# An attention stage's row sums: from sum products on TensorE to ScalarE's accumulator output, with their inverses spread by one product

## The chip, the cores and the metric

The kernel runs on one core of one Trainium2 chip. The metric is the device time of the whole launch in microseconds, the median of several runs. The core's engines are TensorE (PE; its weight loads are listed as PEld), VectorE (DVE), ScalarE (ACT), GpSimd (POOL) and SyncE (SP). Each works through its own queue in order, and they wait for each other by semaphores only.

## The reference

128 images of 176 x 208 pixels become 11 x 13 = 143 patches each, and with a class token S = 144 tokens of 128 features. Two layers follow. The first is a gated convolution and scan, then a mixture of 8 experts (two per token). The second is attention in a window of 32 tokens to each side, 8 heads of 16 features, and one of 16 experts per image. The change concerns the attention:

```python
valid = (idx >= 0) & (idx < S)
scores = jnp.einsum('bshd,bswhd->bshw', q, k_win) * scale
scores = jnp.where(valid[None, :, None, :], scores, -1000000000.0)
attn = jax.nn.softmax(scores, axis=-1)
out = jnp.einsum('bshw,bswhd->bshd', attn, v_win).reshape(B, S, D)
return out @ w_out + b_out
```

The softmax divides each row of exponentials by its sum. Everything is computed in float32.

## The kernel before

The kernel has three stages, one after the other: the first layer up to the routing (to about 1200 us of the profile), the experts' blocks (to about 1880 us), and the third stage, which gathers the experts' results, does the attention and the last experts. The change is in the third.

The third stage goes through the images in 32 steps of 4 images (576 tokens). It is a pipeline written out by hand: `step(v, w, x, y, z)` holds the work of five successive groups of images, each further along. `x` is the group whose attention begins, `y` the one whose attention ends, `v` and `w` are ahead of it (gather, sum and two normalizations, which end in `xq`, the attention's input), `z` is behind it. Each engine has its own `step`, and the order of the calls in it is the order on that engine.

The attention of a group is cut into NU = 9 units of 4 blocks of 16 queries. The 128 partitions of a score tile are 8 heads x 16 queries of a block; its 80 columns are the keys. A unit u goes through these steps:

- GpSimd `diagonal(u)` spreads the queries by head parity (`qdiag`, ring of 3).
- TensorE `scores(u)` (L1540, 16 small products, then the mask by L1548 and L1550) into one of two score banks.
- VectorE `minimum(u)` (L1836) takes the row minimum of the negated scores, `smin`.
- ScalarE `exps(u)` (L1752) makes 4 exponentials of 128 x 80, one per block.
- TensorE `turn(u)` (L1557) transposes them, 4 products; ScalarE `turned(u)` (L1760) copies them to `ex_t` (ring of 3).
- TensorE `values(u)`: 8 products with `pair_ones` (L1570) that sum the exponentials over the keys into `sum_bank`, and then the products with `val` (L1582) into `pv_bank`. Both lie in one PSUM bank, VB.
- VectorE `halves(u)` (L1843 the reciprocal `inv` of the sums, L1844) and `heads(u)` (L1848 `one_head`, L1851 `att`) pick the right half by parity and scale.

Each matmul in float32 appears as two records in the profile. `head_step` counts three VectorE steps per unit, the last of them `one_head`; `values(u)` waits until those of unit u-1 are done, since it writes the bank that they read. Units 0 to 5 of group `x` get their products in its own step, 6 to 8 in the next (as `y`).

GpSimd also issues 12 gathers per step between the `diagonal` calls (L1451), multiplies the gathered rows by the routing weights (L1459) and adds them (L1464, `ysum`). TensorE turns `ysum` (L1510) for `w`'s `prec`. On VectorE the small steps of `pick_expert` (L1959 to L1972) choose `y`'s expert of 16; ScalarE's L1780 makes 4 x 16 exponentials with an accumulator output for it.

## Time and profile before

| what | us |
|---|---|
| median of 3 runs (lowest, highest) | 3124.59 (3123.58, 3134.05) |
| the profiled execution, whole | 3155.56 |
| its span, first to last instruction | 3153.7 |
| TensorE busy in the span | 2771.0 (88%) |
| VectorE busy | 1942.3 (62%) |
| ScalarE busy | 1818.7 (58%) |
| GpSimd busy | 1283.4 (41%) |

Busy time is time in which an engine ran an instruction; waiting on a semaphore is not in it. In the timeline's rows the first number is the start in microseconds from the span's start, the second the time covered, and in brackets stands how long the engine was idle before, and what ended it. "issue" there is time in which the engine waited for nothing that the profile shows. The granted clock is a share of TensorE's full clock.

### The profile page before, as it was taken

To read this page: it belongs to the slowest core of one execution; us is meant where nothing else is said; L and a number is where in the kernel's file an instruction comes from. 1 tells how busy PE (TensorE), PEld (TensorE's weight loads), DVE (VectorE), ACT (ScalarE), POOL (GpSimd) and SP (SyncE) were. 2 spreads that over 40 slices of the span, in tenths; PEclk is the share of its full clock that TensorE was granted. 3 is DMA by queue.
4 is the path that set the end of the run, shared out by engine and by line. 5 is a ranking of instruction groups with operands and counts; after the bars stand their busy time and mean duration, and the time that the engine had idled before them with its cause. 6 is when DMAs were issued, how large, how long until landed. Compare 5 with 4: busy or idle time off the path is not lost.

```text
span 3153.7 us, 84405 instructions
## 1 busy us (share of the span) xinstructions
PE 2771.0 (88%) x30287; PEld 2124.4 (67%) x30287; DVE 1942.3 (62%) x4491; ACT 1818.7 (58%) x3661; POOL 1283.4 (41%) x1252
## 2 busy tenths in 40 slices
PE   6989899989989984999999948888888888888897
PEld 4666666666666663999999936666666666666665
DVE  4788888888777885222222215666666666666665
ACT  4767777767676773444444425555555555555554
POOL 1365555565555555000000045445454444555540
PEclk9999999999999996999999969999999999999998
DMA  3122222222222212777777721111111111111110
GB/s 125 68 92 84 81 80 75 75 91 84 80 81 75 75 31 64 228 230 227 230 229 228 228 75 38 47 46 45 44 44 44 44 44 44 44 45 44 44 34 28
DMA packets 139575, 284.62 MB, mean 90 GB/s; under 512 B 25440, under 2 KB 82784, under 8 KB 135392
## 3 DMA queue, kind: packets, MB, share of 16 engines
q1 hardware_dynamic: 114912, 245.68, 24.3%
q0 software_dynamic: 24576, 37.80, 4.5%
q8 instruction: 53, 0.87, 0.1%
q14 instruction: 34, 0.28, 0.0%
HBM read 215.08 MB, written 68.29 MB: 90 GB/s over the span
## 4 chain that ended last, share of the span: by engine, by line
PE 40%; DVE 8%; issue 7%; POOL 3%; DMA 1%; another core or an unknown queue 1%; ACT 1%; DVEq 0%; SPq 0%; POOLq 0%; ACTq 0%
PE psum L1154 9%; PE psum L1145 8%; PE psum L1540 4%; PE psum L1499 4%; PE psum L1570 2%; PE psum L1582 2%; DVE c L1964 2%; PE psum L1557 2%; PE psum L1516 2%; PE psum L1524 2%; POOL ycho L1451 2%; PE psum L1504 1%; PE psum L1550 1%; PE psum L1136 1%; DVE inv L1843 1%
## 5 line engine op out<-in xcount | busy, mean ns | idle before, releaser
L1451 POOL DMA_INDIRECT ycho<-expert_out,place x384 | 359.3, 936 | 668.5 <-DVE place L1829 585.0
L1019 POOL DMA_INDIRECT expert_in<-rows,slot_i x384 | 445.7, 1161 | 132.3 <-issue 111.5
L1188 ACT ACTIVATE hid<-psum,w_blk 128x256 f32<-128x256 f32 x608 | 268.9, 473 | 326.5 <-PE psum L1145 326.5
L1752 ACT ACTIVATE ex<-psum,smin 128x80 f32<-128x80 f32 x1152 | 281.9, 333 | 204.7 <-DVE smin L1836 204.6
L489 PE MATMUL psum<-xn,w_in 128*128 128x288 f32 x1024 | 306.0, 423 | 33.1 <-issue 12.0
L1472 POOL TENSOR_TENSOR qdiag<-qs,parity 128x128 f32<-128x128 f32 x288 | 114.4, 402 | 507.2 <-PE psum L1550 327.9
L1843 DVE RECIPROCAL inv<-psum 128x64 f32<-128x64 f32 x288 | 158.9, 552 | 240.5 <-PE psum L1582 165.2
L1154 PE MATMUL psum<-w_blk,hid 128*128 128x128 f32 x2432 | 296.6, 275 | 0.0
L1540 PE MATMUL psum<-keys,qdiag 32*32 32x80 f32 x9216 | 267.4, 233 | 31.3 <-issue 22.9
L1145 PE MATMUL psum<-x_t,w_blk 128*128 128x256 f32 x1216 | 289.5, 381 | 2.0 <-DMA w_blk<-w_exp_in 2.0
L995 POOL TENSOR_TENSOR unit<-unit 128x576 f32<-128x576 f32 x64 | 121.9, 1905 | 401.6 <-ACT unit L656 292.7
L1154 PEld LDWEIGHTS psum<-w_blk,hid 128*128 128x128 f32 x2432 | 283.8, 192 | 0.1
L489 PEld LDWEIGHTS psum<-xn,w_in 128*128 128x128 f32 x1024 | 189.4, 194 | 106.5 <-issue 24.0
L1540 PEld LDWEIGHTS psum<-keys,qdiag 32*32 32x32 f32 x9216 | 183.7, 105 | 114.9 <-issue 106.3
L1760 ACT ACTIVATE ex_t<-psum 128x512 f32<-128x512 f32 x288 | 173.7, 603 | 137.0 <-PE psum L1557 129.8
L1145 PEld LDWEIGHTS psum<-x_t,w_blk 128*128 128x128 f32 x1216 | 212.8, 191 | 34.0 <-DMA w_blk<-w_exp_in 2.4
L1252 DVE COPY x_t<-psum 128x256 f32<-128x256 f32 x152 | 64.5, 424 | 230.2 <-PE psum L1136 230.2
L1557 PE MATMUL psum<-cst,ex 128*128 128x128 f32 x1152 | 187.4, 282 | 13.2 <-issue 9.5
L1260 DVE TENSOR_TENSOR rows_out<-psum,w_blk 128x256 f32<-128x256 f32 x152 | 64.5, 424 | 215.7 <-PE psum L1154 215.7
L495 PE MATMUL psum<-xin,w_tok 128*128 128x286 f32 x768 | 195.4, 411 | 2.2 <-DVEq L459 2.2
L1836 DVE TENSOR_REDUCE smin<-psum 128x4 f32<-128x320 f32 x288 | 140.0, 486 | 88.7 <-PE psum L1550 82.5
L495 PEld LDWEIGHTS psum<-xin,w_tok 128*128 128x128 f32 x768 | 145.6, 193 | 50.1 <-issue 10.3
(240 smaller groups left out, 5928.4 us busy)
## 6 DMA issues: line engine op xcount, KB each, us to landing
w_blk<-w_exp_in SPq DMA_DIRECT2D x152, 578.0 KB, 4.0
xin<-x_in SPq DMA_DIRECT2D x32, 1716.0 KB
rows_in<-expert_in SPq DMA_DIRECT2D x152, 128.0 KB, 2.5
expert_out<-rows_out SPq DMA_DIRECT2D x152, 128.0 KB, 3.4
h_dram<-h SPq DMA_DIRECT2D x32, 288.0 KB
x_dram<-x SPq DMA_DIRECT2D x32, 288.0 KB
h1c<-h_dram SPq DMA_DIRECT2D x32, 288.0 KB
x2c<-x_dram SPq DMA_DIRECT2D x32, 288.0 KB
```

Of the source, the lines that this page charges most:

```text
L489: last = nc.tensor.matmul(bank[:, g, 0:T2], w, two(src)[:, g, :], start=True, stop=True)
L495: last = nc.tensor.matmul(bank[:, g, 0:2 * NPATCH], w_tok[:, k, :], xin[x.s][:, k, g * 2 * NPATCH:(g + 1) * 2 * NPATCH], start=(k == 0), s ...
L1019: pool.indirect_dma_start(out=expert_in[:, :], out_offset=bass.IndirectOffsetOnAxis(ap=slot_i[z.s][:, n:n + 1], axis=0), in_=rows[z.s][:, ...
L1145: nc.tensor.matmul(HB[b.s][c % HK], w_blk[b.q][:, c * 128:(c + 1) * 128], x_t[b.s][:], start=True, stop=True).then_inc(hid_done[b.s], 1)
L1154: last = nc.tensor.matmul(YB[b.s][:, t * 128:(t + 1) * 128], hid[b.s][:, c, t * 128:(t + 1) * 128], w_blk[b.q][:, FF + c * D:FF + (c + 1) ...
L1188: nc.scalar.activation(hid[b.s][:, c, :], HB[b.s][c % HK], ACT.Gelu_apprx_tanh, bias=w_blk[b.q][:, FF + FC * D + c:FF + FC * D + c + 1]).t ...
L1451: pool.indirect_dma_start(out=ycho[x.s][:, k, :], out_offset=None, in_=expert_out[:, :], in_offset=bass.IndirectOffsetOnAxis(ap=place[x.s] ...
L1540: nc.tensor.matmul(bank[at, b * QK:(b + 1) * QK], qdiag[u % RING][at, b, :, :].rearrange("p j q -> p (j q)"), keys[at, m, key_range(qb)], ...
L1557: done = nc.tensor.transpose(XB[0:KW, b * 128:(b + 1) * 128], ex[u][:, b, :], C("ident"))
L1752: done = nc.scalar.activation(ex[u][:, b, in_window(qb)], score_bank(u)[:, b * QK:(b + 1) * QK], ACT.Exp, bias=smin[u % RING][:, b:b + 1], ...
L1760: nc.scalar.activation(ex_t[u % RING][:].rearrange("p b r -> p (b r)"), XB[0:KW, :], ACT.Copy).then_inc(ext_ready, 1)
L1843: v.reciprocal(inv[:], sum_bank()).then_inc(head_step, 1)
```

## The change

- ScalarE's exponentials in `exps` get a second output, `accum_out`, the sum of each row, written to `esum` (128 x 4, ring of 3).
- VectorE gets a function `inverses(u)`: the reciprocal `einv` of the 4 columns of `esum`, then a product of `einv`, repeated 16 times, with the constant `block_row` (1 where the column is the partition's query) into `inv_rows` (128 x 64, ring of 3). It is called once per unit, at places of its own in `step`. It counts `inv_step` twice per unit.
- TensorE's 8 products with `pair_ones` are replaced by one product of the constant `head_block` (1 where two partitions belong to the same head) with `inv_rows`. It writes to the same place in PSUM; what stands there is the inverse, spread over the head's 16 rows. Ahead of it TensorE waits for `inv_step`, and for `att_ready` of unit u-1 in place of `head_step`.
- `halves` loses its reciprocal, and `heads` multiplies by `sum_bank()` in PSUM in place of `inv`.
- `exps(u)` waits until `inverses(u-3)` has read its slot of `esum`.
- In `pick_expert`, the subtraction of L1972 becomes a `tensor_tensor` with a repeated operand.

```diff
@@ const_tiles
+        "head_block": (p[:, None] // HD == p[None, :] // HD),
+        "block_row": (p[:, None] % QB == np.arange(QB)[None, :]),
@@ values (TensorE)
                 if u or x.old(1):
-                    pe.wait_ge(head_step, x.upto(HEAD * NU, HEAD * u))
+                    pe.wait_ge(att_ready, x.upto(NU, u))
                 pe.wait_ge(ext_ready, x.upto(NU, u + 1))
-                for j in range(2):
-                    for t in range(NT):
-                        at = slice(t * PH, (t + 1) * PH)
-                        nc.tensor.matmul(sum_bank()[at], pair_ones[:, j, :],
-                                         ex_t[u % RING][:, :, t * PH + j * QB:t * PH + (j + 1) * QB],
-                                         start=(j == 0), stop=(j == 1))
+                pe.wait_ge(inv_step, x.upto(2 * NU, 2 * u + 2))
+                nc.tensor.matmul(sum_bank(), C("head_block"), inv_rows[u % RING][:], start=True, stop=True)
@@ exps (ScalarE)
+                if u >= RING or x.old(1):
+                    act.wait_ge(inv_step, x.upto(2 * NU, 2 * (u + 1 - RING)))
                 for b, (m, qb) in enumerate(blocks(u)):
                     done = nc.scalar.activation(ex[u][:, b, in_window(qb)], score_bank(u)[:, b * QK:(b + 1) * QK],
-                                                ACT.Exp, bias=smin[u % RING][:, b:b + 1], scale=-1.0)
+                                                ACT.Exp, bias=smin[u % RING][:, b:b + 1], scale=-1.0,
+                                                accum_out=esum[u % RING][:, b:b + 1])
@@ VectorE
+            def inverses(x, u):
+                v.wait_ge(ex_ready, x.upto(NU, u + 1))
+                if u or x.old(1):
+                    v.wait_ge(inv_step, x.upto(2 * NU, 2 * u))
+                v.reciprocal(einv[:], esum[u % RING][:]).then_inc(inv_step, 1)
+                v.wait_ge(inv_step, x.upto(2 * NU, 2 * u + 1))
+                if u >= RING or x.old(1):
+                    v.wait_ge(pv_done, x.upto(NU, u + 1 - RING))
+                v.tensor_tensor(inv_rows[u % RING][:], einv[:].unsqueeze(2).to_broadcast([128, UB, QB]),
+                                C("block_row").unsqueeze(1).to_broadcast([128, UB, QB]), ALU.mult).then_inc(inv_step, 1)
@@ halves, heads (VectorE)
-                v.reciprocal(inv[:], sum_bank()).then_inc(head_step, 1)
...
-                                one_head[:], inv[:], ALU.mult).then_inc(att_ready, 1)
+                                one_head[:], sum_bank(), ALU.mult).then_inc(att_ready, 1)
@@ step (VectorE), the calls of inverses, each behind the line given
                     minimum(y, 8)
+                    inverses(y, 7)
...
                     heads(y, 7)
+                    inverses(y, 8)
...
                     minimum(x, 2)
+                    inverses(x, 0)
...
                     minimum(x, 3)
+                    inverses(x, 1)
...
                     minimum(x, 4)
+                    inverses(x, 2)
                     heads(x, 1)
...
                     minimum(x, 5)
+                    inverses(x, 3)
...
                     minimum(x, 6)
+                    inverses(x, 4)
...
                     minimum(x, 7)
+                    inverses(x, 5)
...
+                if x:
+                    inverses(x, 6)
@@ pick_expert (VectorE)
-            v.tensor_scalar(l16[:], l16[:], m16[:, 0:1], None, ALU.subtract).then_inc(pick_step, 1)
+            v.tensor_tensor(l16[:], l16[:], m16[:].to_broadcast([NI, E2]), ALU.subtract).then_inc(pick_step, 1)
```

TensorE, in the loop over the steps, from the scores of unit 3 (L1540 with `keys` and `qdiag`, L1550 the mask) through the products of unit 1 to the transposes of unit 2; REGISTER_ALU and ISA rows carry waits. Before:

```order
L1534 REGISTER_ALU [waits ex_ready]
L1540 MATMUL psum<-keys,qdiag 32x80 [waits qdiag_ready]
L1540 MATMUL psum<-keys,qdiag 32x80 x15
L1550 MATMUL psum<-band,ident_h 128x4x2x16
L1565 REGISTER_ALU
L1570 MATMUL psum<-ex_t,pair_ones 32x64 [waits ext_ready,head_step]
L1570 MATMUL psum<-ex_t,pair_ones 32x64 x7
L1582 MATMUL psum<-ex_t,val 32x64 x8
```

After:

```order
L1534 REGISTER_ALU [waits ex_ready]
L1540 MATMUL psum<-keys,qdiag 32x80 [waits qdiag_ready]
L1540 MATMUL psum<-keys,qdiag 32x80 x15
L1550 MATMUL psum<-band,ident_h 128x4x2x16
L1567 REGISTER_ALU [waits ext_ready,att_ready]
L1568 MATMUL psum<-inv_rows,cst 128x64 [waits inv_step]
L1578 MATMUL psum<-ex_t,val 32x64 x8
L1557 MATMUL psum<-cst,ex 128x128 [waits ex_ready,ext_ready]
```

The sum products between the mask and the products with `val` are gone; in their place stands one product of 128 x 64 that waits for `inv_step`.

VectorE, in the same place of the loop, from the row minimum of unit 3 (`smin`) through `xm` of the group behind and the first part of unit 1 (`inv`, `half`) to the row minimum of unit 4 and unit 1's `one_head`. Before:

```order
L1835 REGISTER_ALU [waits ex_ready]
L1836 TENSOR_REDUCE smin<-psum 128x4 [waits scores_done]
L1910 ISA
L1911 TENSOR_TENSOR xm<-psum,r 128x576 [waits norm5_act]
L1843 RECIPROCAL inv<-psum 128x64 [waits pv_done,att_ready]
L1844 TENSOR_SCALAR half<-psum,parity 128x64
L1835 REGISTER_ALU [waits ex_ready]
L1836 TENSOR_REDUCE smin<-psum 128x4 [waits scores_done]
L1847 REGISTER_ALU
L1848 SCALAR_TENSOR_TENSOR one_head<-psum,parity,half 128x64 [waits head_step]
```

After:

```order
L1834 REGISTER_ALU [waits ex_ready]
L1835 TENSOR_REDUCE smin<-psum 128x4 [waits scores_done]
L1842 RECIPROCAL einv<-esum 128x4 [waits inv_step,ex_ready]
L1843 REGISTER_ALU
L1846 TENSOR_TENSOR inv_rows<-einv,cst 128x64 [waits pv_done,inv_step]
L1923 ISA
L1924 TENSOR_TENSOR xm<-psum,r 128x576 [waits norm5_act]
L1853 TENSOR_SCALAR half<-psum,parity 128x64 [waits pv_done,att_ready]
L1834 REGISTER_ALU [waits ex_ready]
L1835 TENSOR_REDUCE smin<-psum 128x4 [waits scores_done]
L1841 REGISTER_ALU [waits ex_ready]
L1842 RECIPROCAL einv<-esum 128x4 [waits inv_step]
```

The pair that makes `einv` and `inv_rows` for unit 1 stands behind the minimum of unit 3, the pair for unit 2 between the minimum of unit 4 and `one_head` of unit 1, and the reciprocal of 128x64 is gone.

## Rows read from the trace of the kernel before

**Rows 1.** Busy time by engine, third stage: length; PE, PEld, DVE, ACT, POOL; clock; DMA; GB/s.

```profile
1980.00:2941.00 961.00, 847.15 (x16435) 614.06 (x16434) 637.70 (x1662) 538.60 (x1462) 478.38 (x557) 0.98 0.16 45
```

**Rows 2.** The chain that ended last, two steps: start, us, what.

```profile
2400.69 0.83 DVE h L1899
...
2440.82 0.83 DVE h L1899
```

**Rows 3.** Timeline of all engines at the end of a step (see the section on time for columns).

```profile
2417.53 2.75 POOL L1459 TENSOR_TENSOR ycho<-ycho,weights 96x1536 f32<-96x1536 f32 x1 [1.63 <-DMA ycho<-expert_out,place]
2417.59 2.71 DVE L1964 SCALAR_TENSOR_TENSOR c<-l,m,crow 4x16 f32<-4x16 f32 x1
...
2420.36 1.81 POOL L1464 TENSOR_TENSOR ysum<-ycho 96x768 f32<-96x768 f32 x1
...
2420.78 1.42 DVE L1972 TENSOR_SCALAR l<-l,m 4x16 f32<-4x16 f32 x1
...
2423.67 0.43 PE L1570 MATMUL psum<-ex_t,pair_ones 128*32 128x64 f32 x16 [0.73 <-DVE one_head L1848]
...
2425.00 1.24 PE L1516 MATMUL psum<-xq,w_qkv 128*128 128x288 f32 x4 [0.67 <-DVE xq L1949]
```

**Rows 4.** Groups by line and shape, from 1700 us: busy us, mean ns | idle before.

```profile
L1752 ACT ACTIVATE ex<-psum,smin 128x80 f32<-128x80 f32 x1152 | 281.9, 333 | 204.7 <-DVE smin L1836 204.6
...
L1843 DVE RECIPROCAL inv<-psum 128x64 f32<-128x64 f32 x288 | 158.9, 552 | 240.5 <-PE psum L1582 165.2 <-remote 75.2
...
L1976 DVE RECIPROCAL g<-g 4x1 f32<-4x1 f32 x32 | 4.5, 141 | 0.0
```

**Rows 5.** Timeline of PE: sums and products of unit 0.

```profile
2443.42 0.43 PE L1570 MATMUL psum<-ex_t,pair_ones 128*32 128x64 f32 x16
...
2443.67 0.40 PE L1582 MATMUL psum<-ex_t,val 128*32 128x128 f32 x8
```

**Rows 6.** Timeline of PE: a product with 128 weight columns, and the group behind.

```profile
2437.13 0.38 PE L1594 MATMUL psum<-gdiag,cst 4*128 4x4 f32 x2
2437.44 0.76 PE L1540 MATMUL psum<-keys,qdiag 32*32 32x80 f32 x32
```

**Rows 7.** Timeline: last score product of unit 3, unit 1's sums, minimum of unit 3.

```profile
2445.22 0.23 DVE L1851 TENSOR_TENSOR att<-one_head,inv 128x64 f32<-128x64 f32 x1
...
2445.86 0.23 PE L1550 MATMUL psum<-band,ident_h 128*128 128x128 bf16 x1
...
2446.02 0.43 PE L1570 MATMUL psum<-ex_t,pair_ones 128*32 128x64 f32 x16
...
2446.12 0.49 DVE L1836 TENSOR_REDUCE smin<-psum 128x4 f32<-128x320 f32 x1 [0.68 <-PE psum L1550]
```

**Rows 8.** Timeline of ACT: an activation with accumulator output and its read.

```profile
2430.50 0.20 ACT L1780 ACTIVATE p<-l 4x16 f32<-4x16 f32 x1
2430.60 0.18 ACT L1780 ACTIVATION_READ_ACCUMULATOR p<-l 4x1 f32 x1
```

**Rows 9.** Timeline: exponentials of unit 8 and the weight loads of its transposes.

```profile
2428.21 0.98 ACT L1752 ACTIVATE ex<-psum,smin 128x80 f32<-128x80 f32 x4
...
2429.25 0.42 PEld L1557 LDWEIGHTS psum<-cst,ex 128*128 128x128 f32 x4 [0.39 <-ACT ex L1752]
```

**Rows 10.** Timeline: last score product and minimum of unit 4, `one_head` of unit 1, unit 2's sums.

```profile
2448.83 0.22 PE L1550 MATMUL psum<-band,ident_h 128*128 128x128 bf16 x1 [0.36 <-issue]
...
2449.84 0.49 DVE L1836 TENSOR_REDUCE smin<-psum 128x4 f32<-128x320 f32 x1 [1.75 <-PE psum L1550]
...
2450.25 0.27 DVE L1848 SCALAR_TENSOR_TENSOR one_head<-psum,parity,half 128x64 f32<-128x64 f32 x1
...
2450.58 0.43 PE L1570 MATMUL psum<-ex_t,pair_ones 128*32 128x64 f32 x16
```

**Rows 11.** Busy time by engine, single microseconds of one step (columns as rows 1).

```profile
2433.90:2434.90 1.00, 1.00 (x7) 1.00 (x6) 0.87 (x4) 0.37 (x2) 0.85 (x2) 0.50 0.00 0
```

**Rows 12.** PE's waits, 1980 to 2941 us: in total us, times, longest.

```profile
PE psum L1540 <- issue: 18.4, 51, 0.5
```

More of the change, by code:

```diff
@@ L212, in build @@
         band, ident_h = sb("band", [128, cw["band"][1]], BF16), sb("ident_h", [128, 128], BF16)
-        parity, pair_ones = sb("parity", [128, 2]), sb("pair_ones", [KW, 2, 2 * HD])
+        parity = sb("parity", [128, 2])
         place = [sb(f"place{s}", [G, 2 * NG], I32) for s in range(2)]
@@ L1234, in b_vector @@
             v.tensor_reduce(parity[:], C("head_rows").rearrange("p (t j) -> p j t", j=2), AX_X, ALU.add)
-            for j in range(2):
-                v.memset(pair_ones[:, j, j * HD:(j + 1) * HD], 1.0)
-                v.memset(pair_ones[:, j, (1 - j) * HD:(2 - j) * HD], 0.0)
             v.tensor_scalar(q_neg[:], V("q_b"), -float(HD) ** -0.5, None, ALU.mult).then_inc(c_ready, 1)
@@ L1301, in build @@
         smin, ex_t = ring_c("smin", [128, UB]), ring_c("ex_t", [KW, UB, 128])
-        inv, half, one_head = (one_c(name, [128, UB, QB]) for name in ("inv", "half", "one_head"))
+        esum, einv, inv_rows = ring_c("esum", [128, UB]), one_c("einv", [128, UB]), ring_c("inv_rows", [128, UB, QB])
+        half, one_head = (one_c(name, [128, UB, QB]) for name in ("half", "one_head"))
         att = one_c("att", [128, T])
@@ L1322, in build @@
         out_step, out_stored = sem("out_step"), sems("out_stored")
-        zeroed = sem("zeroed")
-        HEAD = 3
+        zeroed, inv_step = sem("zeroed"), sem("inv_step")
+        HEAD = 2
         PICK = 9
```

5 lines of the change are left out of this document (2 added, 3 removed).

## The prediction

> **What bounds the kernel now.** I read the stretches by engine first, then the chain that ended last, then the timeline of one step of the third stage. In 24 steady steps of that stage TensorE is busy 847.15 of 961 us, against 637.70 for VectorE and 538.60 for ScalarE [rows 1]. A step begins anew 40.13 us after the one before (the addition at L1899 starts at 2400.69 and at 2440.82 [rows 2]), and there are 32 steps. So about 0.88 of a step is TensorE's own work, and what matters is where its in-order queue is stopped. Times of rows are given below without their hundreds and thousands (17.53 for 2417.53). In the timeline it stands at few places: it needs `ex` for the transposes of unit 8, `one_head` for the products of unit 2, and at a step's end VectorE's `xq`. That last one hangs on GpSimd: `c` at L1964 has 64 numbers and takes 2.71 us because it starts 0.06 us behind GpSimd's 2.75 us product and ends with it; `l` at L1972 takes 1.42 us and ends with GpSimd's sum (20.36 + 1.81 = 22.17 against 20.78 + 1.42 = 22.20) [rows 3]. From there VectorE has seven instructions up to and with `xq`, and TensorE goes on at 25.00 after 0.67 us of waiting. Ahead of that it waited 0.73 us at unit 5's products [rows 3].
>
> **The change, part by part, per step (9 units).** *TensorE's sums.* Per unit 8 products (16 records) go and one of 128 x 128 weights on 64 columns comes. The old ones overlap, four column groups at once: the sums start at 43.42 and the products behind them at 43.67, so they hold the engine 0.25 us [rows 5]. The nearest row for the new one is L1594, 128 weight columns as well: 0.31 us from its start to the next group [rows 6], an upper bound since its first load was exposed by a wait. From below, the four weight loads of a transpose group take 0.42 us [rows 9], about 0.1 each, so two take 0.2. Between 0.20 and 0.31 against 0.25 I take 0: bounds -0.4 and +0.5 us a step. The Trainium skill's "TensorE: Matmul & The Clock Gate" (LDWEIGHTS) says that a weight load costs its columns over 1.2 GHz, 107 ns for 128; two of them give 0.21, by which the sum would be 0.4 us a step lower. The row with the wait speaks for more, so no term hangs on it.
>
> *VectorE's inversion.* The 128x64 reciprocal goes, 552 ns each [rows 4], 0.46 from its start to the next one's. A reciprocal of 4 numbers comes (141 ns, as that of `g` [rows 4]; 0.18 with the wait behind it) and a 128x64 product (0.23, as `att` [rows 7]; 0.14 until an independent successor starts). VectorE gains 0.14 us a unit, 1.3 a step, nearly all in idle time. In the tail behind GpSimd's sum the old reciprocal (0.46) goes and the pair for unit 5 (0.32) comes: `xq` is 0.1 us earlier. **-0.1.**
>
> *ScalarE's second output.* Each of the 4 exponentials of a unit gets an accumulator read. The one row of that form reads 0.18 us; it starts 0.10 us behind an activation that lasts 0.20 [rows 8], so half of that one overlaps. Neighbouring exponentials overlap likewise: four of 333 ns [rows 4] take 0.98 [rows 9], hence one starts every 0.22 us. I take 0.09 more per exponential: a group takes 1.31 instead of 0.98, that is +0.34; with no overlap at all on either side it would be 2.07, +1.1. ScalarE has room (538.60 of 961 busy), and most groups end well ahead of their transposes. Unit 8's does not: the exponentials run from 28.21 to 29.19, and the weights of its transposes load at 29.25 after waiting for them [rows 9], while the keys' products end there too. **+0.3.**
>
> *The new wait ahead of each unit's products.* TensorE now waits for `inv_step`, so for VectorE's `inverses`; behind that wait stand the unit's products, the next transposes and all later scores. For most units that pair is made long before. For two it can't be: VectorE does `inverses(1)` behind `minimum(3)`, and `inverses(3)` behind `minimum(5)`, while TensorE does `values(1)` directly behind the scores of unit 3 and `values(3)` directly behind those of unit 5. Before, unit 1's products started at 46.02, 0.16 us behind the last score matmul; `smin` of unit 3 can start only at 46.12 [rows 7]. To it come 0.40, the reciprocal 0.18, the product 0.23 and some 0.04 for the signal: 46.97. **+0.95** for `values(1)`, and TensorE has no later idle time before the scores of unit 5, from which GpSimd's gathers, its sum and so `xq` are timed. For `values(3)` the same offsets behind the scores of unit 5 give the same 0.95; but GpSimd's chain is released by then, and TensorE's waits at the step's end, 0.73 and 0.67 [rows 3], take it in: **0** for this one.
>
> *Unit 2.* `inverses(2)` stands between `minimum(4)` and `heads(1)`, and TensorE waits now for `att` instead of `one_head`. Minimum starts at 49.84, `one_head` at 50.25, TensorE at 50.58 [rows 10]. Now, for the signal: 49.84 + 0.40 (minimum) + 0.32 (the pair) + 0.32 (`one_head`) + 0.26 (`att`) = 51.14 against 50.52, +0.6. But that minimum began 1.0 us behind the start of the last score matmul (48.83), where unit 3's began 0.26 behind it, a gap that the trace gives no cause for. Without it the chain through `att` is ready just in time: 0. **+0.3**, the middle of both.
>
> By the same offsets units 0, 4, 6, 7 and 8 have their inverse half a microsecond or more ahead of their products. Unit 5's is ready at 22.17 + 2.1 = 24.3 instead of 23.67, but its products then end where `xq` is due anyway: 0.
>
> The sum: 0.95 + 0.3 + 0.3 - 0.1 = 1.45 us a step, times 32 = **+46 us**. The profiled execution took 3155.56 (span 3153.70, 1.9 around it), so 3202 for its like. It is 31 us above the median of the timed runs, 3124.59; I put the same difference on the median: **3171**. The term bounds (unit 2 at 0 or 0.6, the product -0.4 or +0.5) give 0.75 to 2.25 a step, +24 to +72, 3149 to 3197. A change of 0.5%, 15.6 us, is about what a measurement of this kernel can tell from none.
>
> **The rivals.** *Slower still, by a read that doesn't overlap.* If the accumulator read and the next exponential follow one another (+1.1 a group), the wait at unit 8 grows to 1.1 and the logarithm behind the group of unit 2 is late as well; +0.8 a step over the forecast, 3197. The 0.10 in [rows 8] speaks against it. *Slower, by GpSimd's port.* The new `inv_rows` product reads two tiles of SBUF, as `c` does. For unit 4 it is due about 0.6 us ahead of GpSimd's 2.75 us product, by the same offsets as in [rows 3]. If VectorE comes 0.6 us later than I reckon, it is held to that product's end, the pick's steps move behind the sum, and unit 4's products wait too: about +0.7 a step over the forecast, 3193. "SBUF — State Buffer" of the Trainium skill (Who interferes with whom) states it as a rule: a VectorE instruction with two SBUF inputs is fully blocked by a GpSimd instruction that reads SBUF. By that rule, the trace agrees for `c`, and `inv_rows` is a new instruction of that kind, nine times a step. *Slower, by the clock.* After a stretch in which TensorE was busy about half, its granted clock read 0.50 for some 3 us (the lower level, 1.2 GHz) [rows 11]. Two new idle gaps of 1 us could bring a second such stretch, 1.6 us a step lost in 24 steps, 3210.
>
> *Not slower: stops that go with the removed records.* In the steady steps TensorE stands 18.4 us, in 51 pieces, inside its score products, for nothing that the profile shows [rows 12]; most of it lies in unit 0's scores, and behind that the clock reads 0.50 [rows 11]. The mean clock of 0.98 [rows 1] makes another 2% of 961 us, 19 us. The change takes 126 matmul records and as many weight loads out of some 692 each in a step. If the stops come from the density of instructions and hold outside the profiled execution, they go: 37 us, 3171 - 37 = 3134, within 0.5% of before. If half goes, 3152, in the forecast's range. For it: no engine is waited for there. Against it: the profiled execution is 31 us longer than the timed ones, 1 us a step, so these stops may be the profile's own and have no share in the median.
>
> **How the numbers follow.** Forecast (3149 to 3197) 0.60. The slower rivals: read 0.06, port 0.05, clock 0.05. The stops that go: 0.14, within 0.5%. The stops that go and, with them, VectorE's shorter path to `att` counting where I see idle time: 0.10, faster. That makes faster 0.10, within 0.5% 0.14, slower 0.76. The range reaches from 3130, at the foot of the rival of the stops, to 3205.
>
> **What would show it.** In the profile of the changed kernel: the product of `inv_rows` waits for VectorE about 0.95 us at units 1 and 3 of every step; an accumulator read of about 0.18 us, a group of exponentials of about 1.3 us; the step at about 41.6 us; VectorE's busy time down by some 40 us and ScalarE's up by 1152 x 0.09 = 104 us or more. Wrong would be: no wait at units 1 and 3, a step of 40 us or less, or a wait for `ex` at units other than 8.

## The result, and the profile after

The changed kernel takes 3204.28 us (median of 4 runs, 3203.14 to 3206.73) beside 3126.41 us for the kernel before on the same chip (3123.58 to 3134.05): a ratio of 1.0246, 95% interval 1.0226 to 1.0266. That is +78 us where +46 was forecast; the direction held, and so did the range (3130 to 3205), by 0.7 us. The profiled execution is at 3203.97 (span 3202.1), 48 us above that of before. The two differences, +48 and +78, are not alike because before's profiled execution (3155.56) lies above all of its timed runs, near the 3153 that before takes on the chips of sets 1 and 3 below, while that of after is one of its timed runs. The rows below therefore explain the difference of the profiles and not quite that of the medians. The third stage alone, counted from the first copy of gather places to the end of the span, went from 1315.2 to 1380.3 us: +65. The stages ahead of it were 17 us shorter in this profile, and the change does not touch them.

Chain of work, the same addition in three successive steps, as [rows 2]:

```profile
2370.01 0.83 DVE h L1910
...
2409.74 0.83 DVE h L1910
...
2452.90 0.83 DVE h L1910
```

The first pair is 39.73 us apart and the second 43.16. It goes on like this: in the middle of the stage, steps of 39.7 or 39.8 us take turns with steps of 43.0 to 44.9, where before's are all between 38.6 and 40.7. So every second step is dear, and the cheap ones are about as long as before's. From the first to the last of the 32 the mean distance is 40.77 us (1915.6 to 3179.5), against 38.73 before (1929.9 to 3130.6): +2.04 us a step. The pair in [rows 2], 40.13, was a long one.

Busy time by engine in 961 us of the third stage, columns as [rows 1]:

```profile
1980.00:2941.00 961.00, 807.77 (x12634) 601.30 (x12632) 592.28 (x1780) 583.44 (x2219) 447.54 (x533) 0.96 0.14 43
```

TensorE is busy 39 us less than in [rows 1], at a clock of 0.96 instead of 0.98. So both its idle time and its slow time grew. Its waits in that stretch (in total us, times, longest):

```profile
PE psum L1568 <- DVE inv_rows L1846: 67.8, 78, 1.3
PE psum L1524 <- DVE prec L1885: 33.0, 11, 3.3
PE psum L1504 <- DVE h L1910: 20.4, 23, 0.9
...
PE psum L1557 <- ACT ex L1750: 4.6, 13, 0.4
```

The first row is the new wait, the second one that nobody had forecast. In before's list the corresponding places were 19.5 us for `half` and `one_head`, 12.9 for `xq`, 11.3 for `ysum` and 40.5 for "issue" in all (126 stops). `xq` and `ysum` are no longer in the list, and "issue" is 23.2.

Timeline around the products of unit 1 and, eight microseconds on, of unit 3:

```profile
2414.72 0.23 PE L1550 MATMUL psum<-band,ident_h 128*128 128x128 bf16 x1
2414.99 0.49 DVE L1835 TENSOR_REDUCE smin<-psum 128x4 f32<-128x320 f32 x1 [1.06 <-PE psum L1550]
...
2415.40 0.17 DVE L1842 RECIPROCAL einv<-esum 128x4 f32<-128x4 f32 x1
...
2415.60 0.24 DVE L1846 TENSOR_TENSOR inv_rows<-einv,cst 128x64 f32<-128x64 f32 x1
2415.89 0.43 PE L1568 MATMUL psum<-inv_rows,cst 128*128 128x64 f32 x2 [0.94 <-DVE inv_rows L1846]
...
2423.86 0.43 PE L1568 MATMUL psum<-inv_rows,cst 128*128 128x64 f32 x2 [0.94 <-DVE inv_rows L1846]
```

The steps of the sum stand here one by one: minimum 0.41, reciprocal 0.20, product 0.29 to the start on TensorE, a wait of 0.94 us at each of the two places. Taken over the 961 us, TensorE waited 44 times for 0.94 us (41.4 us in all) at this product, always at units 1 and 3. It also waited 17 times for 1.0 us or more (20.8 us), two of them at units 1 and 3 (1.09 each). The other 15, 18.6 us, are unit 4's:

```profile
2387.60 2.75 POOL L1459 TENSOR_TENSOR ycho<-ycho,weights 96x1536 f32<-96x1536 f32 x1 [1.63 <-DMA ycho<-expert_out,place]
...
2387.90 2.52 DVE L1846 TENSOR_TENSOR inv_rows<-einv,cst 128x64 f32<-128x64 f32 x1
...
2390.48 0.43 PE L1568 MATMUL psum<-inv_rows,cst 128*128 128x64 f32 x2 [1.23 <-DVE inv_rows L1846]
```

Unit 4's `inv_rows` lasts 2.52 us in place of 0.24. It starts 0.30 us behind GpSimd's 2.75 us product and ends with it (2390.42 against 2390.35). This is the rival of the port. In the 961 us 23 of the 209 `inv_rows` products last over 0.5 us, 58.0 us in all, so one in each step. Before, it was `c` that was caught there, in 19 of 25 steps ([rows 3]).

ScalarE, the exponentials with their reads (timeline), and then the groups by line and shape from 1700 us:

```profile
2431.09 0.32 ACT L1750 ACTIVATE ex<-psum,smin 128x80 f32<-128x80 f32 x1
2431.30 0.20 ACT L1750 ACTIVATION_READ_ACCUMULATOR ex<-psum,smin 128x1 f32 x1
2431.39 0.33 ACT L1750 ACTIVATE ex<-psum,smin 128x80 f32<-128x80 f32 x1
```

```profile
L1750 ACT ACTIVATION_READ_ACCUMULATOR ex<-psum,smin 128x1 f32 x1152 | 241.3, 209 | 0.0
L1846 DVE TENSOR_TENSOR inv_rows<-einv,cst 128x64 f32<-128x64 f32 x288 | 134.8, 468 | 9.8
L1568 PE MATMUL psum<-inv_rows,cst 128*128 128x64 f32 x576 | 113.8, 281 | 97.4 <-DVE inv_rows L1846 92.6 <-DVE att L1860 2.4 <-issue 1.2
```

A read lasts 0.21 us, and one exponential follows another after 0.30 us instead of 0.22: the forecast of 0.09 each, 1.3 us for a group, was right.

What nobody had forecast stands at the top of every second step:

```profile
2438.55 0.17 DVE L1828 CAST place<-out_rows 96x12 int32 x1 [2.85 <-issue]
2438.79 0.76 DVE L1885 TENSOR_TENSOR prec<-psum,x2c 128x576 f32<-128x576 f32 x1
...
2439.60 1.72 PE L1524 MATMUL psum<-w_qkv,xq 128*128 128x128 f32 x8 [2.89 <-DVE prec L1885]
```

VectorE stands still for 2.85 us with nothing to wait for, right where its loop begins anew, and TensorE waits 2.89 us behind it. The queue that carries instructions tells more. The page's line on it, first of before and then of after (packets, MB, share):

```profile
q14 instruction: 34, 0.28, 0.0%
```

```profile
q14 instruction: 94, 0.77, 0.1%
```

The loop over the steps holds two steps in its body, so it has 16 turns. In the compiled program VectorE's body has 239 instructions before and 291 after, waits and register instructions included. Sixty packets more in 15 further turns is 4 a turn. That reads as a body which was held and is now loaded again each time; set 1 tests it. VectorE's waits in the 961 us show the same stops, 11 of them (12.3 us more stand at `att`, L1860, further on in the loop):

```profile
DVE place L1828 <- issue: 32.3, 11, 3.2
```

And the clock, a single microsecond behind such a stop (columns as [rows 1]):

```profile
2441.00:2442.00 1.00, 1.00 (x7) 0.96 (x7) 0.54 (x3) 0.56 (x1) 0.84 (x2) 0.50 0.85 325
```

I counted the granted clock over the single microseconds from 1820 to 2980 (the sum of 1 minus the clock, so the microseconds lost). Before loses 47.8 us there, of which some 25 at the stage's beginning, and after 81.3. Before has 13 later stretches at half clock, all of 3 or 4 us. After has 23, of which 10 are of 6 or 7 us. In the 961 us of [rows 1] alone it is 18.8 us before and 42.7 after.

### The profile page after: what moved, and what is told of

Read it like the earlier page. It is cut to its first block, busy times and chain, and to the rows that moved or that the text cites. A ratio compares the mean times of both kernels' runs of the same rounds, so it can differ in the third digit from the quotient of the medians.

```text
span 3202.1 us, 78584 instructions
## 1 busy us (share of the span) xinstructions
PE 2765.1 (86%) x26255; PEld 2141.7 (67%) x26255; DVE 1942.1 (61%) x4775; ACT 1918.7 (60%) x4813; POOL 1286.7 (40%) x1252
## 4 chain that ended last, share of the span: by engine, by line
PE 44%; DVE 7%; issue 6%; ACT 2%; POOL 1%; DMA 0%; DVEq 0%; SPq 0%; ACTq 0%; POOLq 0%
PE psum L1156 8%; PE psum L1147 8%; PE psum L1499 6%; PE psum L1540 5%; PE psum L1578 4%; PE psum L1557 3%; PE psum L1524 2%; PE psum L1568 2%; DVE inv_rows L1846 2%; PE psum L1504 2%; DVE c L1983 1%; PE psum L1516 1%; ACT ex L1750 1%; PE psum L1138 1%; PE psum L1548 1%
## 5 line engine op out<-in xcount | busy, mean ns | idle before, releaser
L1750 ACT ACTIVATE ex<-psum,smin 128x80 f32<-128x80 f32 x1152 | 360.3, 330 | 101.3 <-DVE smin L1835 79.1
L997 POOL TENSOR_TENSOR unit<-unit 128x576 f32<-128x576 f32 x64 | 132.8, 2075 | 375.6 <-ACT unit L658 258.8
L1540 PE MATMUL psum<-keys,qdiag 32*32 32x80 f32 x9216 | 245.1, 238 | 9.8 <-issue 6.6
L1750 ACT ACTIVATION_READ_ACCUMULATOR ex<-psum,smin 128x1 f32 x1152 | 241.3, 209 | 0.0
L1853 DVE TENSOR_SCALAR half<-psum,parity 128x64 f32<-128x64 f32 x288 | 80.8, 281 | 260.9 <-PE psum L1578 260.9
L1540 PEld LDWEIGHTS psum<-keys,qdiag 32*32 32x32 f32 x9216 | 180.7, 108 | 81.9 <-issue 73.7
L1568 PE MATMUL psum<-inv_rows,cst 128*128 128x64 f32 x576 | 113.8, 281 | 97.4 <-DVE inv_rows L1846 92.6
```

Of the source, the lines that this page charges most:

```text
L1540: nc.tensor.matmul(bank[at, b * QK:(b + 1) * QK], qdiag[u % RING][at, b, :, :].rearrange("p j q -> p (j q)"), keys[at, m, key_range(qb)], ...
L1568: nc.tensor.matmul(sum_bank(), C("head_block"), inv_rows[u % RING][:], start=True, stop=True)
L1750: done = nc.scalar.activation(ex[u][:, b, in_window(qb)], score_bank(u)[:, b * QK:(b + 1) * QK], ACT.Exp, bias=smin[u % RING][:, b:b + 1], ...
```

## The experiments

Ratios are to the kernel before on the same chip, and hold within a set only. Each set ran on a chip of its own, on which before itself takes 3153.91 us (set 1), 2986.23 (set 2) and 3152.73 (set 3).

### Set 1: the loop body, and the two waits (before 3153.91 us)

**pad26.** The kernel before, with 26 empty semaphore counts a step on VectorE, which makes its body 291 instructions long:

```diff
                 if x:
+                    for _ in range(26):
+                        v.sem_inc(padded, 1)
                     halves(x, 0)
```

> The kernel before, with 26 semaphore increments per step added to VectorE's queue ahead of unit 0's halves, where it idled 0.83 us; nothing waits for them. VectorE's loop body (two steps) grows from 239 to 291 instructions, the length that the change gives it. Theory length (in the changed kernel VectorE stands 3 us at the top of its loop for nothing the profile shows, because a body of this length isn't kept and has to be fetched anew at every turn): 25 to 40 us slower than before, a stop of about 3 us at the first VectorE instruction of every second step, and more instruction packets on that queue (94 against 34). Theory waits (only the new waits for the inverses cost anything): within 0.5% of before, and the stop is not there.

3206.37 us (3199.43 to 3214.95), ratio 1.0157 (1.0124 to 1.0189): **+50 us from instructions that do nothing but lengthen the loop.** The page's instruction queue and the waits of VectorE and of TensorE in 961 us:

```profile
q14 instruction: 91, 0.75, 0.1%
```

```profile
DVE prec L1876 <- issue: 26.5, 10, 2.8
DVE place L1829 <- issue: 20.7, 10, 2.4
```

```profile
PE psum L1524 <- DVE prec L1876: 42.3, 10, 4.7
```

It is the stop of the changed kernel, a little longer (TensorE waits 4.2 us a turn instead of 3.0), with none of its other edits. Part of the 50 can be the time of the 26 instructions themselves; the next kernels and pad12 bound that.

**short.** The change, with `einv` as a ring of 3 and the waits left out that others then make needless. Its VectorE body has 240 instructions:

```diff
             def inverses(x, u):
                 v.wait_ge(ex_ready, x.upto(NU, u + 1))
-                if u or x.old(1):
-                    v.wait_ge(inv_step, x.upto(2 * NU, 2 * u))
-                v.reciprocal(einv[:], esum[u % RING][:]).then_inc(inv_step, 1)
+                v.reciprocal(einv[u % RING][:], esum[u % RING][:]).then_inc(inv_step, 1)
                 v.wait_ge(inv_step, x.upto(2 * NU, 2 * u + 1))
-                if u >= RING or x.old(1):
-                    v.wait_ge(pv_done, x.upto(NU, u + 1 - RING))
...
             def minimum(x, u):
-                if u >= RING or x.old(1):
-                    v.wait_ge(ex_ready, x.upto(NU, u + 1 - RING))
...
             def halves(x, u):
-                if u or x.old(1):
-                    v.wait_ge(att_ready, x.upto(NU, u))
```

> The changed kernel with the same VectorE work in the same order, without four waits per unit that other waits already imply (einv becomes a ring of three for it): its loop body falls from 291 to 240 instructions. Theory length: the 3 us stop at the top of every second step goes, 27 to 37 us faster than the changed kernel, so about 3172 us. Theory waits: within 0.5% of the changed kernel, 3204; the stop was caused by something else, such as the loads of the next images.

3187.74 us (3179.77 to 3193.67), ratio 1.0091 (1.0064 to 1.0118). The queue is back at 36 packets and the stop at the top is gone:

```profile
DVE place L1828 <- issue: 4.2, 11, 0.4
```

```profile
PE psum L1568 <- DVE inv_rows L1840: 68.0, 80, 1.3
```

TensorE waits for `inv_rows` exactly as in the changed kernel (68.0 against 67.8 us). So what is left at 1.0091 is the cost with no reload, +29 us by the ratio: the forecast's own part, and with it the port's wait at unit 4 (14 times, 16.9 us), which the forecast had as a rival. The changed kernel itself was not run on this chip, so its 1.0246 stands beside the 1.0091 only as the ratio of another.

**early.** The change, with `inverses(1)` ahead of `minimum(3)` and `inverses(3)` ahead of `minimum(5)`; the body stays at 291.

```diff
                 if x:
                     heads(x, 0)
+                    inverses(x, 1)
                     minimum(x, 3)
-                    inverses(x, 1)
...
+                    inverses(x, 3)
                     minimum(x, 5)
-                    inverses(x, 3)
```

> The changed kernel with inverses(1) ahead of minimum(3) and inverses(3) ahead of minimum(5), all else alike. Theory waits, as the prediction had it: TensorE's wait for inv_rows at unit 1 (0.95 us) goes and is on the path to GpSimd's sum, the one at unit 3 lies beside idle time; 0.95 x 32 = 30 us faster than the changed kernel, 3174. If both waits were on the path: 60 us, 3144. Rival: TensorE is held at the loop's top and by GpSimd's sum anyway, and the time stays within 0.5% of 3204.

3209.46 us (3196.05 to 3217.39), ratio 1.0163 (1.0124 to 1.0201). The wait for `inv_rows` fell from 67.8 to 21.3 us, and 18.6 us of waiting for `att` came, 14.3 of them at unit 2. What is left of the first lies at unit 5, none of it at units 1, 3 or 4:

```profile
PE psum L1568 <- DVE inv_rows L1846: 21.3, 17, 1.4
```

Unit 4's product now starts just ahead of GpSimd's long one, by some 0.1 us (2485.01 against 2485.12), and that catches `c` instead, in all but one of 24 steps. Behind `c` unit 5's inverse is late. So the hold moved from one instruction to another and cost TensorE about as much. The stops at the top stayed (94 packets).

**early_short.** Both edits together.

> Both edits together, of short and of early. If the stop and the waits add up: 3204 - 32 - 30 = 3142. If each hides behind the other when alone, the two together gain more than the sum of the two alone; if they take turns in the same slack, less. With both gone the rest above 3126 is ScalarE's reads and unit 2, by the prediction 0.5 us a step, 16 us.

3174.85 us (3160.25 to 3181.8, 8 runs), ratio 1.0065 (1.0046 to 1.0083). Against early, the same program but for the body's length, it is 35 us faster (31 by the ratios): a second price of the reload, without padding and on the same chip. Against short it is 13 us faster (8 by the ratios), where the forecast had 30 for the wait at unit 1 alone. TensorE's waits, first of this kernel:

```profile
PE psum L1568 <- DVE att L1852: 16.6, 24, 0.8
PE psum L1568 <- DVE inv_rows L1840: 12.2, 13, 1.4
```

The waits for `inv_rows` and `att` fell from 68.0 to 28.8 us, 39.2 less. Of that 17.1 us came back as "issue" (32.6 in short, 49.7 here, over all lines) and 5.4 as a wait for `ysum`. On this chip TensorE makes short stops of 0.2 to 0.5 us for which the profile shows no cause, and it made more of them when it was held less elsewhere: 100 in short, 140 here.

### Set 2: the reads, the padding, and the version without waits (before 2986.23 us)

**pad12.** Before, with 12 empty counts a step; the body has 263 instructions.

> The kernel before with 12 semaphore increments per step on VectorE's queue: a loop body of 263 instructions, between 239 (kept) and 291 (fetched anew at each turn). If the edge is at 256 instructions, this one stops at the loop's top as pad26 did (ratio 1.016, some 90 instruction packets on the queue); if it lies above 263, ratio 1.000 and some 35 packets.

2987.3 us (2980.41 to 2995.39), ratio 1.0002 (0.9988 to 1.0017), 35 packets. So 263 instructions are still held, and 12 counts a step cost nothing measurable. That speaks for the reload as nearly all of pad26's 50 us, as do the 35 us between early and early_short. It is not quite shown: 26 counts were never run in a body that is held, and this chip is another, on which TensorE waits for GpSimd in each step.

**after_ctl.** The changed kernel itself, on this chip.

> The changed kernel once more, unchanged, beside the others of this set: the ratio to before should be 1.0246 again, between 1.020 and 1.028. On the chip of the first set, where before took 3154, that would put it at some 3230, so that early (3209) had gained 20 us on it and short (3188) 42 us.

3125.67 us (3123.58 to 3127.63), ratio **1.0461** (1.044 to 1.0481), where the first chip gave 1.0246. Waits in 961 us:

```profile
PE psum L1569 <- DVE inv_rows L1847: 77.4, 71, 1.4
PE psum L1525 <- DVE prec L1886: 22.1, 10, 3.2
PE psum L1511 <- POOL ysum L1465: 11.7, 25, 1.9
```

The expectation, 1.020 to 1.028, was missed by far. The waits at units 1 and 3 and the stop at the loop's top are those of the first chip. But GpSimd's long product catches `c` here (22 times in 24) and not unit 4's `inv_rows`, and the third wait for `inv_rows` is unit 5's: 22 times, 30.3 us, about 1.4 each, where the forecast had 0. Before differs as well. pad12, which stands for it here (1.0002 of its time), has no "issue" stops but waits 69.7 us for `ysum` (its list is below), and of that wait 11.7 are left: so the new waits did replace something, only less than they are. Over 24 middle steps TensorE's idle time is 2.5 us a step in pad12 and 5.0 in the changed kernel, and what it loses to the clock 0.4 and 2.8; the step goes from 34.4 to 39.4 us. On the first chip the same sums are 4.6 and 6.6, 0.9 and 1.9.

**accum_only.** Before, with the accumulator output on every exponential and nothing else:

```diff
                     done = nc.scalar.activation(ex[u][:, b, in_window(qb)], score_bank(u)[:, b * QK:(b + 1) * QK],
-                                                ACT.Exp, bias=smin[u % RING][:, b:b + 1], scale=-1.0)
+                                                ACT.Exp, bias=smin[u % RING][:, b:b + 1], scale=-1.0,
+                                                accum_out=esum[u % RING][:, b:b + 1])
```

> The kernel before, with the second output of ScalarE's exponentials written to esum and read by nobody; the sums are still made by TensorE. Only the accumulator reads are added, 1152 of them. By the prediction (0.09 us more per exponential, on the path at unit 8 alone, 0.3 us a step): 10 us slower, ratio 1.003. Rival, no overlap: 35 us or more, 1.011. Rival, no place where it matters: 1.000.

3067.72 us (3045.15 to 3070.06), ratio **1.0271** (1.0251 to 1.0291): eight times what was expected. Its waits and its 961 us, and then those of pad12:

```profile
PE psum L1511 <- POOL ysum L1465: 64.5, 27, 2.6
PE psum L1558 <- ACT ex L1753: 7.4, 26, 0.3
```

```profile
1880.00:2841.00 961.00, 883.98 (x17809) 663.71 (x17808) 700.77 (x1786) 661.36 (x2540) 538.25 (x605) 0.95 0.17 48
```

```profile
PE psum L1510 <- POOL ysum L1464: 69.7, 28, 2.7
```

```profile
1880.00:2841.00 961.00, 890.66 (x18814) 676.84 (x18813) 735.27 (x1880) 611.24 (x1668) 567.71 (x641) 0.99 0.18 50
```

The only new wait in the list is the forecast's 0.3 us at unit 8, yet the clock is 0.95 instead of 0.99. The steps, from one addition `h` to the next, tell the two costs apart. Of 24 middle steps 20 have no half clock in pad12, and those last 33.8 to 34.2 us. In accum_only only 7 have none, and those last 34.8 to 35.0; 6 with some 3 us of half clock last 36.2 to 36.4, and 11 with some 7 us last 37.5 to 37.7. So the reads alone cost 0.8 us a step, 26 us in 32, and the rest of the 58 us between the two profiled executions goes with the half clock. (accum_only's profiled execution is its fastest run, 23 us below its median.) The 0.8 is more than unit 8's 0.3 because a second group is late, unit 3's, by a gap too short for the list of waits. Its transposes, and the addition ahead of them, in such a step of accum_only and then of pad12:

```profile
2566.47 0.82 DVE L1901 SCALAR_TENSOR_TENSOR h<-psum,att_bias,h 128x576 f32<-128x576 f32 x1 [1.25 <-PE psum L1500]
...
2575.10 0.63 PE L1558 MATMUL psum<-cst,ex 128*128 128x128 f32 x4
```

```profile
2527.18 0.82 DVE L1899 SCALAR_TENSOR_TENSOR h<-psum,att_bias,h 128x576 f32<-128x576 f32 x1 [1.06 <-PE psum L1499]
...
2535.53 0.60 PE L1557 MATMUL psum<-cst,ex 128*128 128x128 f32 x4
```

They start 8.63 us behind it with the reads and 8.35 without. Both kernels wait some 2.5 us for `ysum` at the step's end. In pad12 the clock mostly stays at 1.00 through that stop. In accum_only it often falls:

```profile
2219.00:2220.00 1.00, 0.55 (x4) 0.55 (x5) 1.00 (x3) 0.09 (x1) 0.40 (x1) 0.50 0.26 66
```

**best.** early_short, with `inverses(2)` ahead of `minimum(4)` and `inverses(4)` ahead of `minimum(5)` too.

> early_short, and besides inverses(2) ahead of minimum(4) and inverses(4) ahead of minimum(5): unit 1's att is no longer behind the pair for unit 2, and unit 4's product of two SBUF tiles is far from GpSimd's long product. By the prediction's unit 2 term 0.3 us a step, 10 us faster than early_short (ratio to before 1.0065 there), so 1.003; if GpSimd's port was costly as well, 10 us more and level with before. Rival: both lie beside idle time, 1.0065.

3047.54 us (3044.96 to 3058.83), ratio 1.0212 (1.0183 to 1.024). In its 961 us TensorE does not wait once for `inv_rows` or `att` ahead of the new product, and still it is 2.1% slower than before. Its clock there is 0.94; by the count it loses 85.9 us to it, 40 more than pad12. So against the changed kernel 78 us are regained. What remains looks like accum_only's cost: its two middle steps without half clock last 34.6 and 34.7 us, the 22 others 35.8 to 37.4.

### Set 3: which wait, and which read (before 3152.73 us)

**accum_again.** accum_only once more.

> The kernel before with the accumulator output on all 1152 exponentials and nothing else changed; nobody reads the sums. A repetition, beside the next kernel. In the earlier run of it the third stage's granted clock was 0.95 (0.99 in the padded kernel on the same chip) and TensorE waited 0.3 us for the exponentials at unit 8's transposes in 26 steps. Theory A (that wait lengthens TensorE's idle time at the end of a step, and half clock follows more often) and theory B (the reads delay it in other places, or the half clock comes by where the steps fall) both expect about 1.027 on a chip like the one before, and 1.005 to 1.01 on one where before itself already falls to half clock in each step.

3152.19 us (3148.22 to 3158.36, 12 runs), ratio **1.0001** (0.999 to 1.0011). On this chip 1152 accumulator reads cost nothing. The wait at unit 8 is there in 13 of 24 steps:

```profile
PE psum L1560 <- ACT ex L1755: 3.9, 13, 0.3
```

**accum_no8.** The same, with no accumulator output in unit 8:

```diff
-                                                accum_out=esum[u % RING][:, b:b + 1])
+                                                **({} if u == NU - 1 else {"accum_out": esum[u % RING][:, b:b + 1]}))
```

> As the kernel ahead of it, but the four exponentials of unit 8 have no accumulator output, so the only group whose transposes waited for it is as long as before (0.98 us in place of 1.33). Theory A expects the wait at unit 8 gone, the half clock as rare as in before, and a ratio of 0.998 to 1.004. Theory B expects the wait gone but the half clock still there: 10 us less than the kernel ahead of it (32 x 0.3), and no more.

3160.65 us (3155.38 to 3166.07, 12 runs), ratio 1.0026 (1.0015 to 1.0037). The wait for `ex` is gone (0.6 us in 2 steps), and the kernel is slower than the one that has it, by 0.25%, not faster. On this chip the wait costs nothing that can be measured. The count of the clock says 59.7 us here and 44.4 in accum_again. Theory A of the expectations can't be decided on this chip, since the loss it was to explain did not appear; on the chip of set 2 it was not tried.

**short_e1** and **short_e3.** short with only `inverses(1)` moved ahead of its minimum, and with only `inverses(3)` moved.

> The change with rings and fewer waits, so that VectorE's loop body has 240 instructions, and inverses(1) ahead of minimum(3); inverses(3) stays behind minimum(5). The forecast has the whole of the cost at unit 1 (0.95 us a step, 30 us) and none at unit 3: it expects this one 25 to 30 us faster than the next kernel. If both waits are on the path alike, the two are equal within 5 us. If neither is much on it (the pair of kernels with both and with none moved differed by 8 to 13 us), equal too, and both near the faster of that pair.

> As the kernel ahead of it, but inverses(3) is moved ahead of minimum(5) and inverses(1) stays behind minimum(3). The forecast has nothing at unit 3, so it expects the time of the version with neither moved, 25 to 30 us above the kernel ahead of it. If both waits cost alike, equal to it within 5 us; if only unit 3's is on the path, this one is the faster by 10 us.

short_e1 takes 3194.16 us (3185.01 to 3205.66), ratio 1.0135 (1.0114 to 1.0157); short_e3 3169.06 (3162.64 to 3175.46), ratio 1.0057 (1.004 to 1.0073). **The order is the reverse of the forecast's**: the kernel without the wait at unit 1 is 25 us slower than the one without the wait at unit 3. The comparison is not pure: in both TensorE's waits at unit 4 are gone as well, and in short_e3 `inv_rows` is caught by GpSimd's product only 7 times instead of 23. One step of short_e1 on TensorE, the stops only:

```profile
2429.36 0.43 PE L1568 MATMUL psum<-inv_rows,cst 128*128 128x64 f32 x2 [0.74 <-DVE att L1852]
2433.11 0.43 PE L1568 MATMUL psum<-inv_rows,cst 128*128 128x64 f32 x2 [0.94 <-DVE inv_rows L1840]
2434.88 0.34 PE L1540 MATMUL psum<-keys,qdiag 32*32 32x80 f32 x4 [0.30 <-issue]
2435.65 0.21 PE L1586 MATMUL psum<-w_g,means 128*4 128x16 f32 x2 [0.16 <-issue]
```

and one of the microseconds behind them:

```profile
2436.00:2437.00 1.00, 1.00 (x12) 0.67 (x15) 0.93 (x5) 0.00 (x0) 0.32 (x1) 0.50 0.00 0
```

With unit 1's wait gone, unit 2 waits for `att` (0.74), and unit 3's 0.94 comes 3.8 us behind that. Behind those two the clock stands at half from within 2435 to 2442, in this step as in nearly all: 23 of its 27 later stretches are of 6 or 7 us, where short_e3 has 17 of 3 or 4. The rows of the 961 us, short_e1 and then short_e3:

```profile
1980.00:2941.00 961.00, 852.35 (x12880) 628.49 (x12878) 606.78 (x1816) 592.11 (x2258) 455.15 (x540) 0.92 0.15 43
```

```profile
1980.00:2941.00 961.00, 834.24 (x13263) 620.18 (x13265) 615.81 (x1862) 606.40 (x2320) 481.93 (x555) 0.97 0.16 44
```

short_e1 is idle 18 us less and yet slower. It loses 110.9 us to the clock by the count, short_e3 54.6. Half clock of 6 or 7 us in nearly every step goes with the slower kernel, though it idles less. How many microseconds of idle time there are matters less here than where they lie.

## Why the prediction held, and where its sum failed

The direction was right, and the mechanism named for it is there: VectorE's `inverses` came too late for TensorE, twice a step. But it is the smaller part of the cost. Without the reload the change costs some 29 us (short), where 46 were forecast, and some 50 us (pad26) come from a cause that is not in the prediction. That the two add up to a time inside the range, 0.7 us below its end, is luck, and so is the chip: on that of set 2 the same program is 139 us slower than before. The misses went in both directions.

- **The wait at units 1 and 3: right as a wait.** 0.95 forecast, 0.94 measured, at both places in each step. Its parts, 0.40 + 0.18 + 0.23 + 0.04 from [rows 7] and [rows 4], came out at 0.41 + 0.20 + 0.29.
- **Its weight in time: not right.** The forecast gave unit 1 all of it and unit 3 none. Taking both away gave 8 to 13 us of 30 in set 1, since TensorE's "issue" stops ([rows 12]) and the wait for `ysum` took back 22.5 of 39.2 us. Taking away unit 1's alone, in place of unit 3's, cost 25 us by the clock. The step of the forecast that failed is the one that adds a wait to the end of the step with no look at what it replaces and what clock follows.
- **Unit 5, 0:** 0.33 us in 17 steps of the changed kernel, where unit 4's wait had come ahead of it, but about 1.3 in early and 1.4 in after_ctl, where `c` was caught by GpSimd. The forecast had its inverse 0.6 us late and counted on the wait for `xq` to take that in.
- **Unit 2, +0.3 (0 or 0.6): 0 in the changed kernel.** Its product started unexposed (2420.17). Once unit 1 no longer waits, the wait for `att` is there (0.74), so the upper price, 0.6, was the real one, hidden by the other wait.
- **The reads, +0.09 each and 0.3 at unit 8: right as durations.** That no other group matters was wrong on the chip of set 2, where unit 3's is 0.28 us late too. Their cost was 0 in set 3 (accum_again) and 81 us in set 2 (accum_only), so no single number holds for the term.
- **TensorE's product, 0: too low.** From its start to the next group's it is mostly 0.26 us unexposed and 0.36 behind a wait (88 of some 200), against 0.25 for the old sums ([rows 5]): +0.6 us a step, a little over the upper bound of +0.5. The Trainium skill's "TensorE: Matmul & The Clock Gate" (LDWEIGHTS) had given 0.21 for the two weight loads. The trace agrees with its rate, since they start 0.11 us apart, but the second one's record alone lasts 0.19, so that they take 0.30 together; the row decides.
- **TensorE's other work fell.** Over 24 middle steps the idle time rose by 1.95 us a step and the clock's loss by 1.1, together 3.0, where the step grew by 2.1. Some 0.9 us a step were saved. Most of it stands in the score products: from 1700 us on those of L1540 are busy 267.4 us before and 245.1 after, 0.7 a step, for the same 9216 records. Why they take less isn't shown. (The prediction's count of some 692 records a step is off: the trace has 674, and 548 after, 126 less as it says.)
- **The rival of the port, given 0.05: it came.** An `inv_rows` was caught in every step, 15 times with 1.1 to 1.3 us of waiting on TensorE at unit 4, 18.6 us in 961, 0.8 us a step where 0.7 was priced. It is also why VectorE's busy time, forecast to fall by some 40 us, did not (1942.3 before, 1942.1 after). By the rule in "SBUF — State Buffer" of the Trainium skill, that an instruction of VectorE with two inputs from SBUF is blocked by a GpSimd instruction that reads SBUF, this had to be expected; the trace agrees, 2.52 us in place of 0.24. In early it happened once in 961 us; `c` was caught instead, and unit 5 paid.
- **The rival of the clock, given 0.05: it came in part.** 33.5 us more were lost to the clock than before, in the count over the third stage. Part of it falls behind the stops at the loop's top, so it is not a cost of the two waits alone.
- **The rival of the stops that go:** in the profile they went from 40.5 to 23.2 us in 961, about 0.7 us a step back. It softened the loss and did not turn it.
- **Not in the prediction at all: the reload of VectorE's loop.** The change adds 52 instructions to the body, most of them waits. Somewhere above 263 and at 291 at the latest the body stops being held, and each turn costs a stop of 3 us. It shows in the steps too: of each pair one is as long as before's and the other 3.3 us or more longer. By that, the forecast's own sign of being wrong, "a step of 40 us or less", came true for half of the steps. The direct prices are 50 us (pad26) and 35 us (early against early_short); in the changed kernel TensorE waits 33.0 us in 961 for it. It is the largest single price measured beside the +78, and the order of the instructions, from which the count comes, lay open before the run. "Runtime: NRT & Kernel Launch" of the Trainium skill (Instruction fetch mechanics) says that an engine holds two blocks of 256 instructions and that a taken branch to outside of them forces a load before the engine goes on. The runs agree in kind: a loop of 239, 240 or 263 instructions can lie within two such blocks, and the 60 further packets carry 0.49 MB, 33 KB a turn. That the one of 291 lay across three is an inference that no run shows. Nor was a loop of the same length moved to another place in the program, so the runs don't tell length from place.

Put together for the changed kernel's own profile and that of before, in microseconds a step: waits for `inv_rows` and `att` in place of those for `half`, `one_head`, `xq` and `ysum` +1.05 (68.8 less 43.7, over 24 steps), the stop at the loop's top +1.4 (33.0 over 24), waits for `ex` +0.2, clock +1.1, "issue" -0.7, TensorE's work about -0.9. That is +2.15 where 2.14 was measured over the same steps (2.04 over all 32); the last term was itself found as a difference, so this is bookkeeping and no proof.

**What stays open.** Why stops of the same length go with half clock in one kernel and not in another (accum_only and pad12, both some 2.5 us for `ysum`) was not settled, and so neither was why the reads cost 2.7% on one chip and nothing on another. What causes the short "issue" stops on some chips isn't known. Nor is there a version that beats before: the nearest, short_e3 and early_short, are at 1.0057 and 1.0065 on chips of one kind, best at 1.0212 on the other.

## What to carry to other kernels

Count the instructions of each engine's loop body before and after an edit, waits included: a body that is no longer held costs microseconds in every turn, on an engine that looks half idle. When a product is made ready on a second engine, place its making ahead of whatever else waits for the same event there, and check what GpSimd runs at that moment. Judge a wait by the time of a kernel that lacks it, not by its length, since other stops and the clock give it back or add to it, and try that on more than one chip.

## What the runs showed of the hardware

- A VectorE loop of 263 instructions runs with 35 packets on its instruction queue, one of 291 with 91 to 94 in 16 turns, and then VectorE stops for 2.9 us (the changed kernel) or 4.7 (pad26, at two places together) at each turn.
- An accumulator output adds a read of 0.21 us, of which 0.12 lies beside the exponential: 0.30 us from one to the next instead of 0.22.
- Chips differ by kind: the kernel before takes 2986 us on that of set 2 and 3126 to 3154 on the others. In its profile, at 3156, TensorE makes 126 "issue" stops in 961 us, 40.5 us in all; pad12 on the faster one has none in its list. A change's ratio differs with it, 1.0246 and 1.0461 for the same program.
- Two stops of 0.74 and 0.94 us, the second 3.8 us behind the first, were followed by 6 or 7 us at half clock in nearly every step (short_e1), while a single stop of about 2.5 us in pad12 mostly was not.
- A GpSimd product of 2.75 us held the VectorE product of two SBUF tiles that started just behind it: unit 4's `inv_rows` (2.52 us in place of 0.24) in the changed kernel, `c` in before, early and after_ctl.
